# One core, a block of layers behind a modulated norm: the fill of the pipeline is ordered anew

## What is computed

```python
mod = (_silu(L0_c) @ L0_wmod).reshape(L0_c.shape[0], 6, 1, -1)
sa, ca, ga, sb, cb, gb = (mod[:, 0], mod[:, 1], mod[:, 2], mod[:, 3], mod[:, 4], mod[:, 5])
ga = (2 * (ga >= 0) - 1) * jnp.maximum(jnp.abs(ga), 0.25)
gb = (2 * (gb >= 0) - 1) * jnp.maximum(jnp.abs(gb), 0.25)
h = _layernorm(x, axis=-1) * (1 + ca) + sa
x = x + ga * attn(h)          # 8 layers, below
h = _layernorm(x, axis=-1) * (1 + cb) + sb
x = x + gb * ffn(h)           # 2 shared and 8 routed experts, best 2 of 8

# one of the 8 layers
q, k, v = x @ Wq + bq, x @ Wk + bk, x @ Wv + bv
Q, K = elu(q) + 1, elu(k) + 1
KV, Ksum = sum(K * v), sum(K)                 # over the rows of a sequence
V = Q * KV / (Q * Ksum + 1e-6)
x = layernorm(gelu(V @ Wo + bo) + x)
x = layernorm(gelu(gelu(x @ Wf1 + bf1) @ Wf2 + bf2) + x)
```

## Time and profile before

| | |
|---|---|
| median of 3 runs | 539.97 us (539.44 to 540.39) |
| profiled execution | 542.1 us, of which 540.3 us are the span from its first to its last instruction |
| mean granted TensorE clock | 0.989 |
| busy in the span | TensorE 507.2 us (94%), VectorE 434.7 (80%), ScalarE 407.7 (75%), POOL 295.2 (55%) |
| loads | 9.96 MB read, most of it before 17 us |

### The profile page before, as it was taken

The page is one execution under the profiler, slowest core; times in us unless marked ns, Lnnn a source line. Parts: engine busy times, 40 slices in busy tenths (PEclk is TensorE's granted clock), DMA queues, the critical chain, the costliest instruction groups (busy, mean ns, idle before and its releaser), DMA issues.

```text
span 540.3 us, 8177 instructions
## 1 busy us (share of the span) xinstructions
PE 507.2 (94%) x1958; PEld 307.4 (57%) x1958; DVE 434.7 (80%) x1638; ACT 407.7 (75%) x594; POOL 295.2 (55%) x322
## 2 busy tenths in 40 slices
PE   2879999999999999999999999999999986999996
PEld 2335555565555556555555555555546565777784
DVE  4767988888888888889888888888887575977753
ACT  1748887888888888888888788888887555575752
POOL 3226556655565566555655665556545573555552
PEclk9979999999999999999999999999999998999999
DMA  7200000001000100100010010001000000000000
GB/s 245 82 0 16 6 21 20 15 5 39 15 5 5 34 15 5 39 15 0 5 39 15 5 36 18 0 5 39 0 2 0 1 1 2 0 19 2 20 13 28
DMA packets 15911, 11.22 MB, mean 21 GB/s; under 512 B 8189, under 2 KB 13693, under 8 KB 15893
## 3 DMA queue, kind: packets, MB, share of 16 engines
q1 hardware_dynamic: 15316, 10.42, 6.9%
q10 hardware_dynamic: 576, 0.60, 0.4%
HBM read 9.96 MB, written 1.05 MB: 20 GB/s over the span
## 4 chain that ended last, share of the span: by engine, by line
PE 80%; DVE 11%; issue 3%; POOL 2%; ACT 2%; DMA 1%; SPq 0%; ACTq 0%; DVEq 0%; POOLq 0%
PE bank L413 19%; PE bank L404 14%; PE bank L295 12%; PE bank L427 5%; PE bank L401 5%; PE bank L331 4%; PE bank L336 4%; PE bank L332 4%; PE bank L511 2%; PE bank L513 2%; PE bank L512 2%; PE bank L571 1%; DMA x<-in_x 1%; PE bank L556 1%; PE bank L559 1%
## 5 line engine op out<-in xcount | busy, mean ns | idle before, releaser
L413 PE MATMUL bank<-hid,wf 128*128 128x512 f32 x256 | 120.4, 593 | 0.0
L830 POOL TENSOR_TENSOR rsD<-veD,c_half 128x4 f32<-128x4 f32 x32 | 37.8, 1180 | 104.3 <-DVE veD L931 104.3
L404 PE MATMUL bank<-x,wf 128*128 128x512 f32 x192 | 93.0, 593 | 0.0
L698 ACT ACTIVATE hid<-bank,vbf 128x512 f32<-128x512 f32 x128 | 77.6, 693 | 0.3 <-PE bank L404 0.3
L902 POOL TENSOR_TENSOR xs_lo<-sc,xs_hi 128x512 fp32r<-128x512 f32 x36 | 47.8, 1327 | 46.9 <-ACT xs_hi L798 46.9
L413 PEld LDWEIGHTS bank<-hid,wf 128*128 128x128 f32 x256 | 46.0, 190 | 46.0 <-issue 30.6
L404 PEld LDWEIGHTS bank<-x,wf 128*128 128x128 f32 x192 | 35.1, 190 | 33.2 <-issue 16.2
L985 DVE TENSOR_SCALAR x<-bank,vln 128x256 f32<-128x256 f32 x64 | 31.9, 540 | 26.5 <-PE bank L295 26.5
L945 DVE TENSOR_SCALAR xhB<-bank,meanB,rsB 128x128 f32<-128x128 f32 x128 | 43.7, 405 | 7.8 <-POOL rsB L830 7.8
L945 DVE TENSOR_SCALAR xhD<-bank,meanD,rsD 128x128 f32<-128x128 f32 x128 | 43.7, 405 | 6.9 <-POOL rsD L830 2.7
L848 POOL TENSOR_TENSOR y<-g,xs 128x512 f32<-128x512 f32 x32 | 40.7, 1272 | 13.6 <-ACT g L692 13.5
(11 more groups left out here) (157 smaller groups left out, 1186.9 us busy)
## 6 DMA issues: line engine op xcount, KB each, us to landing
wf<-in_w_f SPq DMA_DIRECT2D x16, 256.0 KB, 2.6
wu<-in_w_unit SPq DMA_DIRECT2D x10, 192.0 KB
wqkv<-in_w_qkv SPq DMA_DIRECT2D x7, 192.0 KB, 2.4
x<-in_x SPq DMA_DIRECT2D x4, 256.0 KB, 6.7
out<-ot SPq DMA_DIRECT2D x4, 256.0 KB, 2.1
wo<-in_w_o SPq DMA_DIRECT2D x8, 64.0 KB, 1.8
wmod<-in_w_mod ACTq DMA_DIRECT2D x1, 384.0 KB, 4.0
vln<-in_v_ln SPq DMA_DIRECT2D x16, 1.0 KB, 1.7
```

The costliest lines, as they stand in the source:

```text
L404: mm = nc.tensor.matmul(ps_ff[j][:], wf1[:, j * P:(j + 1) * P], x2[(c - 2) % CH][:], start=True, stop=True)
L413: mm = nc.tensor.matmul(ps_f0[:], wf2[:, j, :], hid[:, j, :], start=(j == 0), stop=(j == FJ - 1))
L698: nc.scalar.activation(hid[:, j, :], ps_ff[j][:], ACT.Gelu_apprx_tanh, bias=vbf1[:, j:j + 1]).then_inc(h_ready, 1)
L830: nc.gpsimd.tensor_tensor(rs[buf(k, n)][:], ve[buf(k, n)][:], c_half[:], ALU.pow).then_inc(rstd_ready[k], 1)
```

## The change

- TensorE starts with ten products of zeros (`sel` as cleared by POOL) into `ps_v`, then makes only shift and scale of the first norm, then four identity transposes, chunk 0, and then the other four modulation vectors into `ps_d`.
- `wmod` is loaded in two parts, the second (256 KB) as the fifth load of ScalarE's queue; silu waits for `ct` alone; the exp and ln table is loaded right behind silu.
- VectorE normalises chunk 0 at once, then copies shift and scale, then does the statistics of chunks 1 and 2, normalises chunk 1, and enters slot 0. The statistics of chunk 3 go into slot 0, normalising chunk 2 and the variance of chunk 3 into slot 1 ahead of `vt`, normalising chunk 3 into slot 1 behind the statistics of `y1`. The gates are copied in slot 1 and worked out in slot 2.
- TensorE transposes chunk 1 in slot 0, chunk 2 in slot 1 and chunk 3 in slot 2 (banks `ps_f1`, `ps_f0`, `ps_d`); ScalarE follows in the same slots, chunk 2 at the end of slot 1.
- In slots 0 to 2 q goes ahead of v on TensorE, and on VectorE keys times values go ahead of the statistics of `y1`. The transposes of `y1` of item 0 move from the end of slot 1 to the start of slot 2; slot 1 has twelve identity transposes where they were.
- `wqkv_hi`, `xs_hi`, `wqkv_lo` and `xs_lo` are made earlier in slot 2. In the loop the order is what it was.

```diff
...
+        first_bank = [ps_f0, ps_f1, ps_f0, ps_d]
...
@@ -296,15 +297,6 @@
                 mm.then_inc(done, 1)
 
 
...
             def keep_awake(n, out_bank):
 
                 for _ in range(n):
@@ -312,13 +304,28 @@
 
             def first_to_fm(c):
                 pe.wait_ge(normed["I"], c + 1)
-                transposes([ps_f0, ps_f1, ps_b, ps_d][c], rows_of("I", c), to_fm["I"])
-
-            def rest_to_fm():
-                for c in range(1, CH):
-                    first_to_fm(c)
-
+                if c == CH - 1:
+                    pe.wait_ge(mod_copied, 2)
+                transposes(first_bank[c], rows_of("I", c), to_fm["I"])
+
+            def modulate(out_bank, ms):
+                for m in ms:
+                    mm = nc.tensor.matmul(out_bank[:, m * NB:(m + 1) * NB], wmod[:, m * D:(m + 1) * D], sct[:],
+                                          start=True, stop=True)
+                mm.then_inc(mod_mm, 1)
+
+            pe.wait_ge(padded, 1)
+            zeros = sel[:, 0:P].bitcast(F32)
+            for _ in range(10):
+                nc.tensor.matmul(ps_v[:, 0:P], zeros, zeros, start=True, stop=True)
+            pe.wait_ge(ld["const"], 16)
+            pe.wait_ge(ld["mod"], 16)
+            pe.wait_ge(silu_c, 1)
+            modulate(ps_y, (0, 1))
+            keep_awake(4, ps_v)
             first_to_fm(0)
+            pe.wait_ge(ld["gates"], 16)
+            modulate(ps_d, (2, 3, 4, 5))
 
             def slot(s, c, l, extra=None):
                 a, b, f, d = s, s - 1, s - 2, s - 3
...
+                if isinstance(s, int) and s == 2:
+                    pe.wait_ge(y1_ready, 1)
+                    transposes(ps_b, y1, to_tm["B"])
                 if has(a):
                     pe.wait_ge(x_ready, a + 1)
                     if plain(a):
@@ -351,16 +365,19 @@
                     km = qkv_high("k", ps_k)
                     if plain(a):
                         km.then_inc(k_mm, 1)
+                    if plain(a):
+                        if has(a - 1):
+                            pe.wait_ge(elu_q, a)
+                        qkv_high("q", ps_q).then_inc(q_mm, 1)
                     if has(a - 1):
                         pe.wait_ge(kv_ready, a)
                     vm = qkv_high("v", ps_v)
                     if plain(a):
                         vm.then_inc(v_mm, 1)
-                    if has(a - 1):
+                    else:
                         pe.wait_ge(elu_q, a)
-                    qm = qkv_high("q", ps_q)
-                    if plain(a):
-                        qm.then_inc(q_mm, 1)
+                        qkv_high("q", ps_q)
+                run(extra, "behind the products")
                 if has(f):
                     pe.wait_ge(normed["B"], f + 1)
                     transposes(ps_b, xh["B"], to_fm["B"])
@@ -422,8 +439,6 @@
                     if (c - 1) % CH == 0:
                         pe.wait_ge(ld["wo"], 4 * b + 16)
                     wait(pe, x2_ready, HB * b)
-                    if isinstance(b, int) and b == 0:
-                        pe.wait_ge(x_ready, CH)
                     nc.tensor.matmul(ps_b[:], wo[:], vt[(c - 1) % CH][:], start=True, stop=True).then_inc(wo_mm, 1)
                 if has(d) and not has(b):
                     last_norm_to_tm()
@@ -434,9 +449,8 @@
                 if has(f):
                     ff2(0)
                 run(extra, "middle")
-                if has(b):
-                    pe.wait_ge(y1_ready, b + 1)
-                    transposes(ps_b, y1, to_tm["B"])
+                if has(b) and not (isinstance(s, int) and s == 1):
+                    first_norm_to_tm()
                 if has(d):
                     pe.wait_ge(normed["D"], d + 1)
                     transposes(ps_d, xh["D"], to_fm["D"])
@@ -445,7 +459,13 @@
                     ff2(2)
                     ff2(3)
 
-            slots(pe, slot, {"middle": rest_to_fm})
+            def second_fill():
+                pe.wait_ge(mod_copied, 1)
+                keep_awake(12, ps_y)
+
+            slots(pe, slot, {"middle": lambda: first_to_fm(1)},
+                  {"behind the products": lambda: first_to_fm(2), "before ff2": second_fill},
+                  {"behind the products": lambda: first_to_fm(CH - 1)})
 
 
             last = NI - 1
@@ -628,25 +648,23 @@
         @block.scalar
         def _(act):
 
-            act.dma_start(ct[:], c_t).then_inc(ld["mod"], 16)
-            act.dma_start(wmod[:], w_mod).then_inc(ld["mod"], 16)
+            act.dma_start(ct[:], c_t).then_inc(ld["ct"], 16)
+            act.dma_start(wmod[:, 0:2 * D], w_mod[:, 0:2 * D]).then_inc(ld["mod"], 16)
             act.dma_start(wqkv[:], w_qkv[0]).then_inc(ld["wqkv"], 16)
             act.dma_start(va[:], v_a[0]).then_inc(ld["va"], 16)
-            act.wait_ge(ld["mod"], 32)
+            act.dma_start(wmod[:, 2 * D:6 * D], w_mod[:, 2 * D:6 * D]).then_inc(ld["gates"], 16)
+            act.wait_ge(ld["ct"], 16)
             nc.scalar.activation(sct[:], ct[:], ACT.Silu).then_inc(silu_c, 1)
+            nc.scalar.preload_act_table_set(LN_SET)
 
             act.wait_ge(mod_done, 1)
             def first_norm(c):
                 act.wait_ge(to_fm["I"], c + 1)
                 for h in range(HB):
                     b = c * HB + h
-                    ev = nc.scalar.activation(half(xs[c], h), half([ps_f0, ps_f1, ps_b, ps_d][c], h), ACT.Identity,
+                    ev = nc.scalar.activation(half(xs[c], h), half(first_bank[c], h), ACT.Identity,
                                               bias=mod[:, 0, b:b + 1], scale=m1[:, 0, b:b + 1])
                 ev.then_inc(x_ready, 1)
...
@@ -668,7 +686,7 @@
                         act.wait_ge(ld["vbf2"], 4 * d + 16)
                     nc.scalar.activation(g2[:], ps_f0[:], ACT.Gelu_apprx_tanh, bias=vbf2[:, 0:1]).then_inc(g2_ready, 1)
                 run(extra, "start")
-                if (has(a) or has(b)) and not (isinstance(s, int) and s == 1):
+                if (has(a) or has(b)) and not (isinstance(s, int) and s <= 1):
                     nc.scalar.preload_act_table_set(LN_SET)
                 if has(b):
                     act.wait_ge(q_ready, b + 1)
@@ -685,6 +703,7 @@
                 if has(a):
                     act.wait_ge(q_mm, a + 1)
                     nc.scalar.activation(eq[:], ps_q[:], ACT.Exp, bias=va[:, 1:2]).then_inc(eq_ready, 1)
+                run(extra, "before the gelus")
                 if has(b):
                     act.wait_ge(wo_mm, b + 1)
                     if (c - 1) % CH == 0:
@@ -717,8 +736,14 @@
                                                  bias=vln2[:, 1:2], scale=vln2[:, 0:1]).then_inc(x_hi_ready, 1)
                 run(extra, "end")
 
-            slots(act, slot, {"middle": rest_of_first_norm}, None,
-                  {"before the last norm": lambda: (split_qkv_hi(0), first_high())})
+            def last_of_first_norm():
+                first_norm(CH - 1)
+                first_high()
+                split_qkv_hi(0)
+
+            slots(act, slot, {"middle": lambda: first_norm(1)}, {"end": lambda: first_norm(2)},
+                  {"before the gelus": last_of_first_norm})
+            act.wait_ge(gates_done, 1)
             act.wait_ge(ld["moe"], MOE_LOADS)
 
             def second_norm(c):
@@ -829,7 +854,7 @@
                 pool.wait_ge(var_ready[k], n + 1)
                 nc.gpsimd.tensor_tensor(rs[buf(k, n)][:], ve[buf(k, n)][:], c_half[:], ALU.pow).then_inc(rstd_ready[k], 1)
 
-            for c in range(CH):
+            for c in range(CH - 1):
                 rstd("I", c)
 
             def split_x_lo(c, n):
@@ -839,6 +864,7 @@
 
             def slot(s, c, l, extra=None):
                 a, b, d = s, s - 1, s - 3
+                run(extra, "start")
                 if has(d):
                     pool.wait_ge(g2_ready, d + 1)
                     nc.gpsimd.tensor_tensor(y2[:], g2[:], x2[(c - 3) % CH][:], ALU.add).then_inc(y2_ready, 1)
@@ -860,7 +886,6 @@
                 if has(d) and has(s + 1):
                     pool.wait_ge(v_mm, d + 1)
                     split_x_lo((c - 3) % CH, d + 1)
-                run(extra, "last")
 
             def split_weights_lo(us):
                 for u in us:
@@ -868,7 +893,7 @@
                     nc.gpsimd.tensor_tensor(wu_lo[:, u, :, :], wu[:, u, :, :], wu_hi[:, u, :, :].bitcast(F32),
                                             ALU.subtract).then_inc(wu_lo_ready, 1)
 
-            slots(pool, slot, None, None, {"last": lambda: split_x_lo(CH - 1, 0)})
+            slots(pool, slot, None, {"start": lambda: rstd("I", CH - 1)}, {"start": lambda: split_x_lo(CH - 1, 0)})
             slot(NI, 0, LAYERS, {"end": lambda: rstd("F", 0)})
             split_weights_lo(ORDER[:2])
             slot(NI + 1, 1, LAYERS)
@@ -951,29 +976,60 @@
 
             def modulation():
                 dve.wait_ge(mod_mm, 1)
```

(63 more changed lines are left out.)

34 lines of the change are left out of this document (8 added, 26 removed).

## The result

The changed kernel takes **535.48 us** (median of 8 runs, 535.39 to 537.37), the kernel before in the same session 539.71 (8 runs, 537.56 to 541.40). The ratio is 0.9927 with a 95% interval of 0.9905 to 0.9948: 4.2 us faster (8.2 were forecast), and outside the range of 529.7 to 534.9.

A forecast was written before the change was run, and what follows sets the result against it. TensorE bounds loop and tail; the gain lies in the first slots, where VectorE sets the start and the clock falls. 5.5 + 2.3 + 0.4 = 8.2 us off the median 539.97 gives 531.8 us, range 529.7 to 534.9.

The forecast's parts named there:

- Slot 0: First slot: VectorE, not the earlier first product, decides; mk starts at 13.45 instead of 18.96, 5.5 us earlier.
- Slot 1: Second slot: nck at 17.0; VectorE's added 1.75 us fits a 2.04 us wait ahead of vt; all 5.5 us kept.
- Slot 2: Third slot: the clock stays high; transposes of xhB end at 28.7 instead of 36.50, 7.8 us earlier, 2.3 of it new.
- rival A: Slots 1 and 2: the clock falls all the same, 2.6 us given back, 534.4 us; chance 0.14.
- Slot 3: Fourth slot: wqkv_lo and xs_lo are ready early, first product at 37.9 instead of 46.26; 0.4 us more gained.
- They end at 35.2, those start at 35.3: Slot 2: VectorE's second_split and gates end at 35.2, just ahead of the statistics at 35.3, so they cost nothing.
- rival B: Three pieces fitted into waits with 0.3, 0.0 and 0.1 us to spare don't fit; each 0.5 late, 533.2 us; chance 0.13.
- The sum: Whole kernel: 5.5 + 2.3 + 0.4 = 8.2 us, set against the median of 539.97, gives 531.8 us.
- The tail: Loop and code behind it: order unchanged, so no loss; a constant 8.2 us between the traces after slot 3's first product.
- Rival E: Tail: the late low-clock stretch, 3.2 us at half speed, falls away; 1.6 us more gained, 530.2 us; chance 0.08.
- C: Slot 0: gates, fifth on ScalarE's load queue, hold TensorE ahead of k; the 5.5 us go, 537.3 us; chance 0.04.
- D: Loop: moved instruction memory slows each of 7 passes; over 1.17 us each is slower than before, 541.6 at 1.4; chance 0.03.

The follow-up runs named there:

- after_upfront: The changed kernel with VectorE again working off all four chunks ahead of slot 0, chunk 0 still first: 541.27 us, ratio 1.0008.
- before_fills: The kernel before plus only the ten products of zeros at TensorE's start and twelve identity transposes in slot 1: 537.28 us, ratio 0.9947.
- after_2: The changed kernel, unedited, profiled and timed again: 536.46 us, ratio 0.9923 to the kernel before.
- after_pool_2: Second run of the changed kernel with POOL waiting in the expert part's unit 4 until VectorE has normalised the next chunk: 531.96 us, ratio 0.9831.
- after_pool: The changed kernel with POOL waiting in the expert part's unit 4 until VectorE has normalised the next chunk: 530.99 us, ratio 0.9815.
- after_gates: The changed kernel with the gates' seven VectorE operations moved from slot 2 into slot 1: 536.42 us, ratio 0.9935.
- before_2: The kernel before, unedited, profiled and timed again: 539.56 us, ratio 0.9978.
- before_pool: The kernel before with only POOL's wait for VectorE's normalised chunk in the expert part: 537.93 us, ratio 0.9959.
- after_best: The changed kernel plus POOL's wait, gates in slot 1, twelve more identity transposes in slot 2, last y2 transposes later: 530.13 us, ratio 0.9808.

## Why the prediction was right in direction and wrong in size

**Slot 0: right.** mod_done was forecast for 8.0 (measured 7.55 + 0.16), mk for 13.45, measured 12.74; 0.55 of that is that chunk 1 no longer was waited for till 8.38. That deferral and not the earlier product is what counts was right: after_upfront starts its products at 9.52 too, and its loop ends 4.1 later. The clock of slot 0 was to cost at most 0.4 and cost 0.1 or less (vt 18.54 with six products of 4.54, 18.64 with 2.84).

**Slot 1: right.** nck 16.29 and vt 18.54 are 6.22 us earlier each, so third_norm and the variance were hidden in the wait ahead of vt as costed. "Q ahead of V makes eq come one product (0.86 or 1.7) earlier, which was hidden here anyway" was wrong: with the old order (and the low clock in slot 0) eq holds up xs of chunk 1 on ScalarE, nck comes 1.8 us later and the loop ends 2.2 later. It didn't hurt the sum, which let slot 1 keep slot 0's 5.5 us; with the old order, in that execution, slot 1 didn't keep them all.

**Slot 2: right.** Transposes of xhB end at 28.14 (forecast 28.7), 8.36 us earlier than before; 6.22 of it was there at vt, so 2.1 is new in slot 2. It was forecast at 2.3, nearly all of it clock, and before_fills measures 2.2 for the clock. The low clock came back behind them in two of five profiles with TensorE's slot 2 as changed (28.5 to 32.5 in after_2, 29 to 33 in after_pool_2; not in after, after_pool, after_gates), at a cost of 1.0 us at the end of the loop. This is rival A in a milder form and a later place; runs of the kernel after lie in two groups, 535.4 (five) and 536.9 to 537.4 (three), and the low stretches in the traces are what I take for the difference. It isn't shown: the mean clocks on record, 0.992 to 0.996 in the first group and 0.989 to 0.992 in the second, lean that way but overlap. The rule of the Trainium skill that a transpose doesn't count as activity ("TensorE: Matmul & The Clock Gate", Part 4) isn't borne out: the clock stayed at 1.00 behind 28 of them in a row, and in before_fills the fall in slot 2 went away with twelve added, beside the ten products at the start.

**Slot 3: the cover was missed.** The first product came at 36.71, 1.2 earlier than forecast, but then TensorE waited 0.84 us for xhB. "They end at 35.2, those start at 35.3" left out that TensorE could be earlier than forecast while VectorE's queue was not: the statistics stood ready from the transposes of y1 at 34.10 + 0.60, and began at 35.32, right behind the gates. after_gates gets 0.5 us of this back. This is rival B, at the size it was priced for a single piece. By their ends the transposes of xhB are 8.36 us earlier in slot 2 (36.50 to 28.14) and 8.20 in slot 3 (47.76 + 0.60 to 39.50 + 0.66): the 0.4 of slot 3 didn't come, 0.2 was lost instead. That the shift still comes to the forecast 8.2 is luck: slot 0 had brought 6.2 where 5.5 was forecast, 0.55 of the surplus because chunk 1 was in time.

**The sum: right for these two traces, wrong for the kernel.** 8.2 was forecast, 8.14 stands at the end of the loop. The step that failed is "Set against the median of 539.97 the sum gives 531.8". The sum had been worked out from an execution 2.1 above the median, of which I said only that a late low clock might be part. The cause was in a row that I had shown, chunk 1 at 8.38: it is the latest of four profiles with the loads and VectorE's order of before (6.64, 7.50, 7.89, 8.38). The change takes this wait away, so on an execution whose chunk 1 is earlier it takes away less. before_2, whose time is near the median, ends its loop at 393.41, so the change is worth 393.41 - 387.29 = **6.1** us there, 2.0 less than in the first pair: 1.76 of it stands at mk already, behind a landing 1.74 earlier.

**The tail: the step "The loop and the tail are TensorE's, and the change leaves their order alone" failed**, and with it "a constant 8.2 between the two traces". From the end of the loop to the end of the span it is 144.9 in before, 144.8 in before_2 and 146.1 in after, each with one low stretch: **1.3 us** lost, by VectorE and POOL meeting otherwise (with the POOL wait, which keeps them apart, the tails are equal). In the sum the tail stood at nothing, on the ground that its order doesn't change. 6.1 - 1.3 = 4.8 is the difference of before_2 and after (538.2 and 533.4); the medians give 4.2, with an interval of 2.8 to 5.1. The 0.6 between them isn't assigned; before_2's profiled execution is itself 0.7 above its median. The tail of after_2 is 147.6 with two low stretches; a low stretch in the tail costs 1.5 us (143.3 in before_fills without one, 144.8 in before_2 with one), 0.9 with POOL's wait (142.5 in after_pool, 141.6 in after_pool_2). Rival E had one fall away; none did, it moved.

**What stays open.** What decides between the two engines. In the traces without POOL's wait the step is there to see: of the meetings at chunks 2 and 3, POOL waits in all fourteen where it starts 0.06 us behind VectorE's fourth operation, and VectorE in all six where it starts 0.01 behind, which are those of chunk 3 in the kernels with the changed prologue. But at chunk 1 it starts 0.07 behind VectorE's first, and VectorE is the one stretched; and why VectorE's fourth comes 0.05 us later in those six isn't shown. Open too is what makes chunk 1's landing vary by 1.74 us.

C and D did not happen: the products of slot 0 started at 9.52 with the gates fifth on their queue, and from the transposes of xhB in slot 3 to those behind the loop it is 347.67 us before (395.43 - 47.76) and 347.79 after (387.29 - 39.50), so the moved loop body costs 0.1 us at most over all its passes.

## What to carry to other kernels

Before a sum is set against a median, ask how the profiled execution differs from the typical one in just the wait that the change removes: a wait for data can differ, as it did here by 1.74 us, and a second profile of the same kernel tells. Read a shift at a milestone right behind the changed part and again ahead of the tail, and price the tail by its own difference, since code that isn't touched can answer to the shift. And look for operations of VectorE that take twice their usual time beside one of POOL: one wait that kept them apart brought 2.0 us on the kernel before (537.93 against 539.89) and took the tail of the changed one from 146.1 to 142.5.

## What the runs showed of the hardware

- Four fp32 `tensor_scalar` of 128x128 (1.11 us alone) took 2.21 us when the fourth met one POOL `tensor_tensor` of 1.30, and 2.92 beside two of them, of 1.30 and 1.00; a compare of 128x256 took 1.52 instead of 0.41. POOL's `xs_lo` took 1.30 where one of the four was stretched to its end (1.40 us), and 1.44 where it was not; beside the compare both were long (1.50 and 1.52). The Trainium skill ("SBUF — State Buffer", Terms) says of the two engines that they share a pair of ports which one of them holds for a full instruction. That one operation of VectorE takes 1.40 beside POOL's 1.30, and the three ahead of it their usual 0.34, agrees.
- The second 256 KB load of x, with the same loads ahead of it, was there for VectorE at 6.64 in one execution and at 8.38 in another.
- A low stretch of the clock in the tail came and went between executions with the same code there, starting between 441 and 449 or between 501 and 507, at 0.9 to 1.5 us each; before_fills, before_pool, after_pool_2 and after_best had none.
